# Attention probabilities of all four heads turned by 32x32 blocks and moved inside SBUF, instead of two by TensorE and two through DRAM

## The chip, the core and the metric

One core of one Trainium2 chip runs the whole program. The metric is the device time of one execution in microseconds (us); the kernel before is given as the median of three runs.

## What is computed

The input is x, 8 batches of 128 rows of 512 numbers. Stage one is a linear layer with a chosen low-rank adapter and an attention of 32 small heads. Stage three is a linear layer with a gate. The change lies in stage two, an attention with 32 query heads of 128, 8 key/value heads, and a paged cache of 512 old keys and values per batch. For every batch b and group g (one key/value head and its four query heads) it computes, cut to what matters:

```python
q, k, v = x1 @ Wq.T, x1 @ Wk.T, x1 @ Wv.T       # k and v: 128 new rows
q, k = rope(rmsnorm(q) * wq), rope(rmsnorm(k) * wk)
keys, values = concat(cache, k), concat(cache, v)  # 640 rows
p = softmax(mask(q @ keys.T) / sqrt(128))          # 128 x 640 per head
h += (p @ values) @ Wo_part
```

## The kernel before, in words

The order of the work is written out by hand. `slots` (L1180) calls, on each engine, one `slot(m, one, two, last)` for each of the 64 items m (8 groups g by 8 batches b). `one` and `two` are the items one and two ahead, whose queries and keys are prepared meanwhile; `last` is the item behind, whose probabilities are multiplied with the values; `before` is two behind. An engine works off its own list in order, and semaphores join the lists. All products are made of high and low halves (`_h`, `_l`), three matmuls for a full product.

In a slot TensorE (PE) does `scores(m, 1)`, `out(before, 2)` and `out(before, 3)`, `turn_q(one)`, `scores(m, 2)`, `values_of_highs(last)`, `scores(m, 3)`, `values_of_lows(last)`, `turn_new(one)`, `project_q(two)`, `out(last, 0)`, `out(last, 1)`, `scores(one, 0)` and `project_kv(two)`. Between them stand two `turn_probs`.

A head's scores (128 queries by 640 keys) lie in the PSUM banks 0 and 1. VectorE (DVE) takes `minima` (L1618: mask, scale, minimum, into `sm`), ScalarE (ACT) takes `exponent` (L1504: `sm` to `pf`). The result must be turned, keys onto partitions, before the product with the values:

- heads 2 and 3 (`BY_PE`): `turn_probs` on PE (L1347, five 128x128 transposes into banks 2 and 3), the high half by `high` on ACT (L1517), the low half by `low` on DVE (L1640);
- heads 0 and 1 (`BY_DMA`): `turn_blocks` on DVE (L1631, every 32x32 block turned), `blocks_away` on the SP queue to DRAM (L1246), `blocks_back` in four transfers of 80 KB (L1253) that put the blocks in their places, then `high_moved` on ACT (L1522) and `low_moved` on GpSimd (POOL, L1775), both over 640 columns.

The new key of `one` is turned by rope: DVE makes two products in `new_values` (L1600), POOL adds and scales them in `rope_keys` (L1758), PE turns the result in `turn_new` (L1330), ACT and DVE take its halves in `new_keys`. POOL also does `rms` (L1744: two small instructions, the second a power), the low halves of the cached keys and values (L1771, L1767), the rope sum of the queries (L1753), and the low halves of the next group's weights in the slots with b = 0, 1, 5 and 6.

The SP queue issues all transfers, in the order of `slot` at L1262: blocks, cached keys, blocks, cached values, weights.

## Time and profile before

| | |
|---|---|
| runs | 1300.37, 1301.07, 1304.16 us |
| median | 1301.07 us |
| span of the profiled execution, first to last instruction | 1299.0 us |
| busy: PE, DVE, ACT, POOL | 1249.3, 985.6, 837.8, 836.1 us |
| mean granted TensorE clock | 0.984 |

The page of the profiled execution gives its span and no other time of it; the median of the runs is 2.1 us above the span. Busy times are sums over the whole program; the second stage lies from about 265 to 1250 us. In a timeline each row has the start, the duration, the engine, the line of the kernel, the operation, and output<-inputs; what stands in brackets is how long the engine had been idle and what released it. Matmuls of PE are pipelined, so the durations of two that follow each other overlap, and what one costs is the distance between starts.

### The profile page before, as it was taken

To read this page: it belongs to the slowest core of one execution; us is meant where nothing else is said; L and a number is where in the kernel's file an instruction comes from. 1 tells how busy PE (TensorE), PEld (TensorE's weight loads), DVE (VectorE), ACT (ScalarE), POOL (GpSimd) and SP (SyncE) were. 2 spreads that over 40 slices of the span, in tenths; PEclk is the share of its full clock that TensorE was granted. 3 is DMA by queue.
4 is the path that set the end of the run, shared out by engine and by line. 5 is a ranking of instruction groups with operands and counts; after the bars stand their busy time and mean duration, and the time that the engine had idled before them with its cause. 6 is when DMAs were issued, how large, how long until landed. Compare 5 with 4: busy or idle time off the path is not lost. (4 is left out here: it accounts for less than half of the span.)

```text
span 1299.0 us, 26260 instructions
## 1 busy us (share of the span) xinstructions
PE 1249.3 (96%) x7496; PEld 1074.6 (83%) x7496; DVE 985.6 (76%) x2388; ACT 837.8 (64%) x2505; POOL 836.1 (64%) x787
## 2 busy tenths in 40 slices
PE   5799997799999999999999999999999999999988
PEld 4677775688888888888888888888888888888878
DVE  3567857467888878887888778878888888788766
ACT  2667777466767676666766776676666767666731
POOL 1656656475767676758665876687667766775741
PEclk9899998899999999999999999999999999999999
DMA  7546554345455555555555555555555455455441
GB/s 264 204 170 243 206 217 151 104 115 146 133 139 134 140 140 142 143 139 134 146 136 146 137 144 131 139 137 144 134 143 140 131 143 143 126 138 141 134 133 65
DMA packets 288945, 191.48 MB, mean 147 GB/s; under 512 B 151201, under 2 KB 256674, under 8 KB 287778
## 3 DMA queue, kind: packets, MB, share of 16 engines
q1 hardware_dynamic: 287792, 189.64, 51.2%
q8 instruction: 61, 1.00, 0.3%
q14 instruction: 82, 0.67, 0.2%
q10 hardware_dynamic: 1010, 0.17, 0.1%
HBM read 143.60 MB, written 79.69 MB: 172 GB/s over the span
## 5 line engine op out<-in xcount | busy, mean ns | idle before, releaser
L1779 POOL TENSOR_TENSOR b_p_l<-b_moved,b_p_h 128x640 fp32r<-128x640 f32 x128 | 200.9, 1570 | 163.9 <-PE ps L1375 93.8
L1514 ACT ACTIVATE b_pf<-b_sm,b_mn 128x640 f32<-128x640 f32 x256 | 212.4, 830 | 127.5 <-DVE b_mn L1624 127.5
L1624 DVE CUSTOM_DVE_ANT_0 b_sm<-ps,mask_row,b_rstd 128x640 f32<-128x640 f32 x256 | 225.0, 879 | 53.7 <-PE ps L1301 48.8
L1526 ACT ACTIVATE b_p_h<-b_moved 128x640 fp32r<-128x640 f32 x128 | 94.7, 740 | 160.0 <-DMA b_moved<-blocks_of_probs 158.8
L1660 DVE SCALAR_TENSOR_TENSOR b_hacc<-ps,b_ri,b_hacc 128x512 f32<-128x512 f32 x248 | 182.4, 736 | 4.6 <-PE ps L1301 4.3
L1299 PE MATMUL ps<-b_w_h,x1t_h 128*128 128x512 f32 (+1 forms) x512 | 178.8, 349 | 0.1
L1299 PE MATMUL ps<-b_kt_h,b_qt_h 128*128 128x320 f32 x512 | 169.5, 331 | 4.6 <-DVE b_mn L1624 4.2
L1300 PE MATMUL ps<-b_w_l,x1t_h 128*128 128x512 f32 (+1 forms) x512 | 173.4, 339 | 0.0
L1301 PE MATMUL ps<-b_w_h,x1t_l 128*128 128x512 f32 (+1 forms) x512 | 173.2, 338 | 0.0
L1301 PE MATMUL ps<-b_kt_h,b_qt_l 128*128 128x320 f32 x512 | 159.3, 311 | 0.0
L1300 PE MATMUL ps<-b_kt_l,b_qt_h 128*128 128x320 f32 x512 | 159.2, 311 | 0.0
L1644 DVE TENSOR_TENSOR b_p_l<-ps,b_p_h 128x640 fp32r<-128x640 f32 x128 | 104.8, 819 | 41.1 <-ACT b_p_h L1520 41.1
L1638 DVE STREAM_TRANSPOSE b_blk<-b_pf 128x640 f32<-128x640 f32 x128 | 107.8, 842 | 33.6 <-ACT b_pf L1514 33.6
L1769 POOL TENSOR_TENSOR b_v_l<-b_cv,b_v_h 128x512 fp32r<-128x512 f32 x64 | 82.9, 1295 | 57.0 <-ACT b_v_h L1496 56.9
L738 POOL TENSOR_TENSOR a_pr<-a_pr,a_ri 128x512 f32<-128x512 f32 x64 | 68.4, 1080 | 71.9 <-DVE a_ri L603 71.9
L1299 PEld LDWEIGHTS ps<-b_kt_h,b_qt_h 128*128 128x128 f32 x512 | 97.1, 190 | 13.0 <-DVE b_mn L1624 6.5
L1301 PEld LDWEIGHTS ps<-b_w_h,x1t_l 128*128 128x128 f32 x512 | 96.4, 188 | 11.8
L441 ACT ACTIVATE a_pr<-a_sm,a_mn 128x128 f32<-128x128 f32 x256 | 99.1, 397 | 10.7 <-PE ps L308 10.5
L1299 PEld LDWEIGHTS ps<-b_w_h,x1t_h 128*128 128x128 f32 x512 | 96.7, 189 | 9.6 <-issue 0.8
L1299 PE MATMUL ps<-b_wo_h,b_o_h 128*128 128x512 f32 x256 | 101.6, 397 | 2.7 <-DVE b_o_l L1648 1.6
L1300 PEld LDWEIGHTS ps<-b_w_l,x1t_h 128*128 128x128 f32 x512 | 96.8, 189 | 8.6
L1367 PE MATMUL ps<-b_p_h,b_v_l 128*128 128x512 f32 x256 | 102.3, 400 | 0.0
(177 smaller groups left out, 3371.1 us busy)
## 6 DMA issues: line engine op xcount, KB each, us to landing
blocks_of_probs<-b_blk SPq DMA_DIRECT2D x128, 320.0 KB, 2.4
b_moved<-blocks_of_probs SPq DMA_DIRECT2D x512, 80.0 KB, 2.1
kv_of_batch<-in_kv SPq DMA_DIRECT2D x128, 256.0 KB
b_ck<-kv_of_batch SPq DMA_DIRECT2D x64, 256.0 KB, 4.0
b_cv<-kv_of_batch SPq DMA_DIRECT2D x256, 64.0 KB, 1.9
raw<-in_w SPq DMA_DIRECT2D x32, 384.0 KB, 3.2
raw<-in_wo SPq DMA_DIRECT2D x32, 256.0 KB, 2.8
a_xt<-in_xt SPq DMA_DIRECT2D x8, 256.0 KB, 6.7
```

Source lines behind the costliest of these rows:

```text
L441: op = act.activation(pr[:, c % 4, j], sm[:, c % 2, j], ACT.Exp, bias=mn[:, h:h + 1], scale=-1.0, accum_out=rs[:, h:h + 1])
L1299: pe.matmul(out, lhs[0], rhs[0], start=start, stop=False)
L1300: pe.matmul(out, lhs[0], rhs[1], start=False, stop=False)
L1301: return pe.matmul(out, lhs[1], rhs[0], start=False, stop=stop)
L1367: mm = pe.matmul(ps[:, OT, :], l, p_h[:, i], start=False, stop=False)
L1514: act.activation(pf[:, h % 2], sm[:, h % 2], ACT.Exp, bias=mn[:, m.b % 2, h:h + 1], scale=-1.0, accum_out=rs[:, m.b % 2, h:h + 1]).then_in ...
L1526: act.activation(blocks_of(p_h[:, :, h * P:(h + 1) * P]), moved[:, d].rearrange("p (a t j) -> p a t j", a=LT, j=QUAD), ACT.Copy).then_inc( ...
L1624: dve.tensor_tensor_reduce(sm[:, h % 2], score_row, mask_row[:, m.b], rstd[:, m.b % 4, h:h + 1], -MASKED, ALU.add, ALU.min, mn[:, m.b % 2, ...
L1638: dve.transpose(by_quadrant(blk[:, d]), by_tile(pf[:, h % 2])).then_inc(blk_sb, 1)
L1644: dve.tensor_tensor(p_l[:, :, cols], turned_row, p_h[:, :, cols], ALU.subtract).then_inc(pl_sb, 1)
L1660: dve.scalar_tensor_tensor(out=hacc[:, m.b], in0=ps[:, OUT[h], :], scalar=share, in1=hacc[:, m.b], op0=ALU.mult, op1=ALU.add).then_inc(h_s ...
L1779: pool.tensor_tensor(blocks_of(p_l[:, :, h * P:(h + 1) * P]), moved[:, d].rearrange("p (a t j) -> p a t j", a=LT, j=QUAD), blocks_of(p_h[: ...
```

## The change

All four heads go one way. `turn_blocks` on DVE turns the blocks of each head and writes a pair of heads into one tile (`blk_first`, `blk_second`). `blocks_across` on the SP queue moves a pair in four transfers of 160 KB from SBUF to SBUF, each from 32 partitions to all 128, with no step through DRAM. ACT and POOL take the high and the low half of a pair in one instruction of 1280 columns each. The keys of a tile come out in another order (partition 4j + c has key 32c + j), so the cached values are loaded and the new keys written in that order.

The exponential writes over `sm`. `minima` of head h then waits until head h-2 has been turned on DVE, and `pf` is gone. The scores use two pairs of banks in turn. `scores(m, 3)` stands right behind `scores(m, 2)`. The sum of the two rope products of the new key moves from POOL to DVE (`key_sum`, both inputs in SBUF), and its scaling from POOL to ACT (`turned_key`). The low halves of the second pair are taken by POOL in the next slot, behind `rms`. Stage three's small tiles get other places.

```diff
+            def blocks_across(m, pair):
+
+                sp.wait_ge(blk_sb, REP * m.n + 2 * (pair + 1))
+                wait(sp, ml_sb, 2 * (m.n - 1) + pair + 1)
+                for a in range(LT):
+                    place = moved[:, pair].rearrange("p (h a n) -> p h a n", h=2, a=LT)[:, :, a]
+                    sp.dma_start(place, blk[pair][a * QUAD:(a + 1) * QUAD, :]).then_inc(moved_in[pair], 16)
 
             def slot(m, one, two, last):
-                if m:
-                    blocks_away(m, 0)
-                    blocks_back(m, 0)
-                    blocks_away(m, 1)
+                blocks_across(m, 0)
                 if two:
                     key_rows(two)
-                blocks_back(m, 1)
-                if two:
-                    value_rows(two)
...
+                blocks_across(m, 1)
+                if two:
+                    value_rows(two)
...
-                wait(pe, mn_sb, REP * m.n + h)
+                wait(pe, mn_sb, REP * m.n + h - 1)
                 q = slice(h * P, (h + 1) * P)
-                for bank, place, keys in ((SC, slice(LEAD, 512), slice(0, CUT)), (SC + 1, slice(0, CUT), slice(CUT, NK))):
+                first = SC[h % 2]
+                for bank, place, keys in ((first, slice(LEAD, 512), slice(0, CUT)), (first + 1, slice(0, CUT), slice(CUT, NK))):
...
-            def turn_probs(m, h):
-                pe.wait_ge(exp_sb, REP * m.n + h + 1)
-                wait(pe, pl_sb, len(BY_PE) * m.n + BY_PE.index(h))
-                for i in range(NT):
-                    mm = pe.transpose(turned_row[:, i], pf[:, h % 2, i * P:(i + 1) * P], ident[:])
-                mm.then_inc(pt_ps, 1)
...
                 scores(m, 2)
+                scores(m, 3)
                 if last:
                     values_of_highs(last)
-                scores(m, 3)
-                if last:
                     values_of_lows(last)
                 if one:
                     turn_new(one)
-                turn_probs(m, 2)
...
-                turn_probs(m, 3)
...
+            def turned_key(m):
+                act.wait_ge(kab2_sb, m.n + 1)
+                act.wait_ge(rstd_sb, m.n + 1)
+                act.activation(ka[:], kb[:], ACT.Copy, scale=rstd[:, m.b % 4, REP:REP + 1]).then_inc(kr_sb, 1)
...
+            def high(m, pair):
+                act.wait_ge(moved_in[pair], 16 * LT * (m.n + 1))
                 wait(act, pvh_ps, m.n)
+                act.activation(pair_of(p_h, pair), moved_pair(pair), ACT.Copy).then_inc(mh_sb, 1)
...
                 exponent(m, 2)
                 if m.b == 6:
                     kv_weights(m.g + 1)
-                high_moved(m, 0)
+                if one:
+                    turned_key(one)
                 if last:
                     output(last)
                 exponent(m, 3)
-                high(m, 2)
+                high(m, 0)
                 if one:
                     new_keys(one)
                     cache_values(one)
-                high_moved(m, 1)
...
+            def key_sum(m):
+                dve.wait_ge(kab_sb, m.n + 1)
+                dve.tensor_tensor(kb[:], ka[:], kb[:], ALU.add).then_inc(kab2_sb, 1)
...
                 if one:
                     new_values(one)
-                if last:
-                    low(last, 3)
+                    key_sum(one)
                 minima(m, 2)
                 turn_blocks(m, 1)
                 if before:
                     accumulate(before, 3)
                 if m.n == end.n:
                     h_rest(dve, 1)
+                minima(m, 3)
                 if one:
                     queries(one)
-                minima(m, 3)
+                turn_blocks(m, 2)
                 if last:
                     output(last)
                     invert(last)
-                low(m, 2)
+                turn_blocks(m, 3)
...
+            def low_probs(m, pair):
+                pool.wait_ge(mh_sb, 2 * m.n + pair + 1)
                 wait(pool, pv_ps, m.n)
+                pool.tensor_tensor(pair_of(p_l, pair), moved_pair(pair), pair_of(p_h, pair), ALU.subtract).then_inc(ml_sb, 1)
 
             def slot(m, one, two, last):
                 if one:
                     rms(one)
-                    rope_keys(one)
+                if last:
+                    low_probs(last, 1)
...
-                low_moved(m, 0)
+                low_probs(m, 0)
                 if one:
                     cache_values(one)
-                low_moved(m, 1)
```

The first place is DVE in an early slot, from the products of the new key to the first product of the queries. Of the kernel before:

```order
L1602 TENSOR_TENSOR b_vn_l<-ps,b_vn_h 128x128
L1605 TENSOR_TENSOR b_ka<-ps,cw 128x128
L1607 TENSOR_TENSOR b_kb<-ps,sw 128x128
L1644 TENSOR_TENSOR b_p_l<-ps,b_p_h 128x5x128
L1624 ISA b_sm,b_mn<-ps,mask_row,b_rstd 128x640
L1624 ISA b_mn 128x1
L1638 STREAM_TRANSPOSE b_blk<-b_pf 128x640
L1612 TENSOR_TENSOR b_qt_l<-ps,b_qt_h 128x512
L1624 ISA b_sm,b_mn<-ps,mask_row,b_rstd 128x640
```

And of the changed kernel:

```order
L1568 TENSOR_TENSOR b_vn_l<-ps,b_vn_h 128x128
L1571 TENSOR_TENSOR b_ka<-ps,cw 128x128
L1573 TENSOR_TENSOR b_kb<-ps,sw 128x128
L1578 TENSOR_TENSOR b_kb<-b_ka,b_kb 128x128
L1595 ISA b_sm,b_mn<-ps,mask_row,b_rstd 128x640
L1595 ISA b_mn 128x1
L1608 STREAM_TRANSPOSE b_blk_first<-b_sm 128x4x160
L1624 SCALAR_TENSOR_TENSOR b_hacc<-ps,b_ri,b_hacc 128x512
L1595 ISA b_sm,b_mn<-ps,mask_row,b_rstd 128x640
L1595 ISA b_mn 128x1
L1582 TENSOR_TENSOR b_qt_l<-ps,b_qt_h 128x512
L1608 STREAM_TRANSPOSE b_blk_second<-b_sm 128x4x160
```

The low half of head 3 has gone from its place behind `b_kb`, and the sum with two SBUF inputs stands there, ahead of the minima of head 2 and of everything that follows them.

The second place is POOL over one slot. Of the kernel before:

```order
L1749 TENSOR_SCALAR b_rstd<-b_ss 128x5
L1751 TENSOR_TENSOR b_rstd<-b_rstd,half 128x5
L1762 TENSOR_TENSOR b_ka<-b_ka,b_kb 128x128
L1765 TENSOR_SCALAR b_ka<-b_ka,b_rstd 128x128
L1773 TENSOR_TENSOR b_kt_l<-b_ck,b_kt_h 128x512
L1779 TENSOR_TENSOR b_p_l<-b_moved,b_p_h 128x4x5x32
L1769 TENSOR_TENSOR b_v_l<-b_cv,b_v_h 128x512
L1779 TENSOR_TENSOR b_p_l<-b_moved,b_p_h 128x4x5x32
L1756 TENSOR_TENSOR b_ra<-b_ra,b_rb 128x512
```

And of the changed kernel:

```order
L1712 TENSOR_SCALAR b_rstd<-b_ss 128x5
L1714 TENSOR_TENSOR b_rstd<-b_rstd,half 128x5
L1732 TENSOR_TENSOR b_p_l<-b_moved,b_p_h 128x8x5x32
L1727 TENSOR_TENSOR b_kt_l<-b_ck,b_kt_h 128x512
L1732 TENSOR_TENSOR b_p_l<-b_moved,b_p_h 128x8x5x32
L1723 TENSOR_TENSOR b_v_l<-b_cv,b_v_h 128x512
L1719 TENSOR_TENSOR b_ra<-b_ra,b_rb 128x512
```

The two instructions on the new key are gone, the low halves are twice as wide, and one of them stands right behind the power of `rms`.

## Rows read from the trace of the kernel before

**Rows 1.** Windows of 40 us, busy time of each engine, granted clock, DMA share.
```profile
280.00:320.00 40.00, 40.00 (x237) 35.52 (x236) 33.21 (x67) 26.00 (x76) 24.67 (x25) 1.00 0.51 134
...
1040.00:1080.00 40.00, 40.00 (x225) 34.93 (x225) 32.03 (x64) 25.71 (x70) 23.90 (x22) 1.00 0.56 143
```

**Rows 2.** Timeline of DVE from the rope of the queries on.
```profile
702.54 0.68 DVE L1598 TENSOR_TENSOR b_rb<-ps,sw 128x512 f32<-128x512 f32 x1
703.14 0.74 DVE L1660 SCALAR_TENSOR_TENSOR b_hacc<-ps,b_ri,b_hacc 128x512 f32<-128x512 f32 x1
704.34 0.88 DVE L1624 CUSTOM_DVE_ANT_0 b_sm<-ps,mask_row,b_rstd 128x640 f32<-128x640 f32 x1 [0.46 <-PE ps L1301]
...
706.22 0.84 DVE L1638 STREAM_TRANSPOSE b_blk<-b_pf 128x640 f32<-128x640 f32 x1 [0.33 <-ACT b_pf L1514]
707.18 0.88 DVE L1624 CUSTOM_DVE_ANT_0 b_sm<-ps,mask_row,b_rstd 128x640 f32<-128x640 f32 x1
...
707.99 0.75 DVE L1660 SCALAR_TENSOR_TENSOR b_hacc<-ps,b_ri,b_hacc 128x512 f32<-128x512 f32 x1
708.65 0.28 DVE L1602 TENSOR_TENSOR b_vn_l<-ps,b_vn_h 128x128 fp32r<-128x128 f32 x1
...
709.05 0.28 DVE L1607 TENSOR_TENSOR b_kb<-ps,sw 128x128 f32<-128x128 f32 x1
...
724.71 0.28 DVE L1607 TENSOR_TENSOR b_kb<-ps,sw 128x128 f32<-128x128 f32 x1
```

**Rows 3.** Timeline of PE: one `turn_probs`, the scores behind it, the lows.
```profile
705.42 0.71 PE L1351 MATMUL ps<-ident,b_pf 128*128 128x128 f32 x5
705.88 0.39 PE L1299 MATMUL ps<-b_kt_h,b_qt_h 128*128 128x320 f32 x1
706.11 0.31 PE L1300 MATMUL ps<-b_kt_l,b_qt_h 128*128 128x320 f32 x1
706.26 0.31 PE L1301 MATMUL ps<-b_kt_h,b_qt_l 128*128 128x320 f32 x1
...
712.78 1.09 PE L1375 MATMUL ps<-b_p_l,b_v_h 128*128 128x512 f32 x4
```

**Rows 4.** Timeline of POOL in the second stage.
```profile
702.70 1.57 POOL L1779 TENSOR_TENSOR b_p_l<-b_moved,b_p_h 128x640 fp32r<-128x640 f32 x1 [0.16 <-ACT b_p_h L1526]
704.24 1.29 POOL L1756 TENSOR_TENSOR b_ra<-b_ra,b_rb 128x512 f32<-128x512 f32 x1
706.63 0.20 POOL L1749 TENSOR_SCALAR b_rstd<-b_ss 128x5 f32<-128x5 f32 x1 [1.11 <-ACT b_squares_out L1475]
706.91 1.19 POOL L1751 TENSOR_TENSOR b_rstd<-b_rstd,half 128x5 f32<-128x5 f32 x1
...
730.96 2.40 POOL L1737 TENSOR_TENSOR b_w_l<-raw,b_w_h 128x1024 fp32r<-128x1024 f32 x1
```

**Rows 5.** Timeline of DVE in the first stage: instructions with both inputs in SBUF.
```profile
80.42 1.07 DVE L572 TENSOR_TENSOR a_qr<-a_rope_a,a_rope_b 128x512 f32<-128x512 f32 x1
...
94.11 0.68 DVE L871 TENSOR_TENSOR sw<-t_minus_sine,t_norms 128x512 f32<-128x512 f32 x1
```

**Rows 6.** Timeline of POOL in the first stage, at the same times.
```profile
79.90 1.04 POOL L738 TENSOR_TENSOR a_pr<-a_pr,a_ri 128x512 f32<-128x512 f32 x1
80.90 1.75 POOL L724 TENSOR_TENSOR a_kr<-a_rope_a,a_rope_b 128x512 f32<-128x512 f32 x1
```

**Rows 7.** Timeline of the SP queue: four transfers from DRAM back, one head.
```profile
709.27 1.74 SPq L1260 DMA_DIRECT2D b_moved<-blocks_of_probs  x4
```

**Rows 8.** DMA issues of the page: KB of each, median us from issue to landing.
```profile
b_moved<-blocks_of_probs SPq DMA_DIRECT2D x512, 80.0 KB, 2.1
...
b_ck<-kv_of_batch SPq DMA_DIRECT2D x64, 256.0 KB, 4.0
```

**Rows 9.** Timeline of ACT: copies of 640 and of 1024 columns.
```profile
712.60 0.74 ACT L1526 ACTIVATE b_p_h<-b_moved 128x640 fp32r<-128x640 f32 x1 [0.78 <-DMA b_moved<-blocks_of_probs]
...
727.45 1.05 ACT L1456 ACTIVATE b_w_h<-raw 128x1024 fp32r<-128x1024 f32 x1
```

More of the change, by code:

```diff
@@ L932, in phase3 @@
     ht_h, ht_l = (x1t_l[:, 4], x1t_l[:, 5]), (x1t_l[:, 6], x1t_l[:, 7])
-    b_gate = sb("b_gate", [P, NR])
-    first = sb("first", [P, NR])
+    b_gate, first = small_rows[:, 0:NR], small_rows[:, NR:2 * NR]
+    sc, weight = [small_rows[:, 8 * (1 + i):8 * (2 + i)].rearrange("p (k r) -> p k r", k=2) for i in range(2)]
+    top, expert = small_rows[:, 24:26], small_rows[:, 26:28]
     most = sb("most", [P, 2, MAXR])
-    sc = sb("sc", [P, 2, NR])
-    top = sb("top", [P, 2])
-    weight = sb("weight", [P, 2, NR])
-    expert = sb("expert", [P, 2])
-    low = sb("low", [P, 2, 2, MAXR])
     lowt = sb("lowt", [P, 2, P], F32R)
@@ L948, in phase3 @@
     bth_sb, btl_sb = sem("bth_sb"), sem("btl_sb")
-    small = ((b_gate, "b_gate"), (first, "first"), (most, "most"))
+    small = ((b_gate, "b_gate"), (first, "first"), (most[:], "most"))
     def flat(ap):
@@ L1074, in choose @@
         dve.wait_ge(top_sb, b + 1)
-        dve.scalar_tensor_tensor(out=weight[:, k], in0=sc[:, k], scalar=top[:, k:k + 1], in1=first[:],
+        dve.scalar_tensor_tensor(out=weight[:, k], in0=sc[:, k], scalar=top[:, k:k + 1], in1=first,
                                  op0=ALU.is_ge, op1=ALU.mult).then_inc(weight_sb, 1)
@@ L1155, in phase2 @@
         hacc = sb("hacc", [P, B, D])
[L1156 to L1157 removed]
+        blk_second = sb("blk_second", [P, 2 * NK])
+        blk = (blk_first, blk_second)
+        moved = sb("moved", [P, 2, 2 * NK])
         const_sb = sem("const_sb")
@@ L1170, in phase2 @@
         mn_sb, exp_sb, ri_sb = sem("mn_sb"), sem("exp_sb"), sem("ri_sb")
-        ph_sb, pl_sb = sem("ph_sb"), sem("pl_sb")
-        blk_sb, blk_out, moved_in = sem("blk_sb"), [sem(f"blk_out{h}") for h in BY_DMA], [sem(f"moved_in{h}") for h in BY_DMA]
+        blk_sb, moved_in = sem("blk_sb"), [sem(f"moved_in{pair}") for pair in range(2)]
         mh_sb, ml_sb = sem("mh_sb"), sem("ml_sb")
@@ L1212, in blocks_of, with pair_of, moved_pair, head_in_pair @@
         def blocks_of(ap):
-            return ap.rearrange("p t (a j) -> p a t j", a=LT)
+            return ap.rearrange("p t (b j) -> p b t j", j=QUAD)
+        def pair_of(tile, pair):
+            return blocks_of(tile[:, :, pair * 2 * P:(pair + 1) * 2 * P])
+        def moved_pair(pair):
+            return moved[:, pair].rearrange("p (b t j) -> p b t j", b=2 * LT, j=QUAD)
+        def head_in_pair(h):
+            return blk[h // 2][:].rearrange("p (c h t j) -> p h c t j", c=LT, h=2, j=QUAD)[:, h % 2]
+        def by_block(ap):
+            return ap.rearrange("p (j c) -> p c j", c=LT)
         block = ctx.enter_context(nc.Block())
@@ L1541, in slot @@
                 if last:
-                    high(last, 3)
+                    high(last, 1)
                 exponent(m, 1)
@@ L1579, in slot @@
                     exponent(one, 0)
-            scalar_first(act, (q_weights, kv_weights, squares, new_kv, queries, cache_keys, new_keys, cache_values))
+            scalar_first(act, (q_weights, kv_weights, squares, new_kv, queries, turned_key, cache_keys, new_keys, cache_values))
             slots(act, slot)
-            high(end, 3)
+            high(end, 1)
             h_out(act, 2)
@@ L1710, in low_kv_weights @@
                 dve.tensor_tensor(w_l[:, :, cols], raw[:, :, cols], w_h[:, :, cols], ALU.subtract).then_inc(wkvl_sb, 1)
-            vector_first(dve, (rope_products, new_values, queries, new_keys, minima, low_weights, low_kv_weights))
+            vector_first(dve, (rope_products, new_values, key_sum, queries, new_keys, minima, low_weights, low_kv_weights))
             slots(dve, slot)
             accumulate(end.before(), 2)
-            low(end, 3)
             accumulate(end.before(), 3)
@@ L1808, in _ @@
             pool.wait_ge(const_sb, 1)
-            gpsimd_first(pool, (q_weights, kv_weights, rope_queries, rms, rope_keys, cache_keys, cache_values))
+            gpsimd_first(pool, (q_weights, kv_weights, rope_queries, rms, cache_keys, cache_values))
             slots(pool, slot)
+            low_probs(end, 1)
             pool_ffn(pool)
```

116 lines of the change are left out of this document (29 added, 87 removed).

## Prediction

> **What bounds it now.** I read the windows first. From 280 to 1080 us PE is busy for 40.00 of every 40 us, twenty windows long, at a clock of 1.00 [rows 1]. DVE is busy for 32 to 33 of them, ACT and POOL for 24 to 30. The timelines then give the period: `b_kb` starts at 709.05 and again at 724.71, so a slot takes **15.66 us** [rows 2], and 64 of them are nearly the whole second stage. PE never waits in a slot. So whatever PE is spared is won in full, as long as no other engine needs more than the new slot. That condition is what has to be worked out.
>
> **What PE is spared.** Five turns take 0.46 us (705.42 to 705.88), and the matmul behind them holds the next one for 0.23 us where its like takes 0.15 (705.88 to 706.11, 706.11 to 706.26) [rows 3]. That is 0.54 per `turn_probs`, 1.09 for two. `turn_new`, which stood ahead of one of them, now pays its own 0.08. PE saves 1.0 us, and its slot would be **14.65 us**; over some 62 slots that is -62 us. The second pair of score banks and the moved `scores(m, 3)` issue the same matmuls and remove no wait, since there is none: nothing.
>
> **DVE.** Per slot two `low` of 640 columns go and two block turns of 0.84 us come [rows 2], both about 0.75 from start to start: nothing. `key_sum` is new, 128 columns like `b_kb`, 0.20 from start to start. DVE then needs about 12.7 of 14.65 us.
>
> **ACT.** Four copies of 640 columns become two of 1280. A copy takes 0.74 for 640 and 1.05 for 1024 columns [rows 9], so 1.26 for 1280, an estimate along that line: a little less in all. `turned_key`, 128 columns, comes in. ACT stays under 11 us of a slot; nothing by itself.
>
> **POOL.** A low half takes 1.57 for 640 columns, 1.29 goes for 512 and 2.40 for 1024 [rows 4]. Along that line 1280 columns take 2.96, and the next starts after 2.93. Two of them, three instructions of 1.27 (keys, values, rope sum of the queries) and `rms` with the power (0.37 and 1.18) make 11.2 us. Weights add 12.6 us in eight slots (eight pieces of 1.27 and one of 2.4). That is 12.8 of 14.65 on average, but in slots 0, 5 and 6 of each group it runs over, and the next `low_probs(last, 1)` is late.
>
> **The transfers.** Per pair four transfers of 160 KB replace, for two heads, a trip to DRAM and eight transfers of 80 KB. Four take 1.74 us to issue, 1.31 to the start of the last [rows 7]. From issue to landing the near row says 2.1 us (80 KB), the far one 4.0 (256 KB, of smaller packets) [rows 8]; I take 2.4, near the first, since the packets keep their kind and only their number doubles. The Trainium skill gives a reason for more ("SBUF — State Buffer", Door 1: The DMA port swizzle): of SBUF's 16 DMA ports 32 partitions reach only 8, and it states 189 GB/s measured there. By that figure, as an estimate, four such transfers need 3.5 us, and the landing would be 3.5. No row here shows a read from 32 partitions.
>
> **The wait that the change brings.** In the second stage no DVE instruction of before has both inputs in SBUF. In the first stage some do, and there the rows show what happens beside POOL. Such an instruction of 512 columns takes 0.68 us (L871) [rows 5]. The one at 80.42 took 1.07: POOL was inside an instruction from 79.90 to 80.94, and the DVE one ended 0.55 after that [rows 5, 6]. POOL's next instruction, begun at 80.90, in turn took 1.75. So whoever is first holds the other up to its end. The Trainium skill says the same as a rule ("SBUF — State Buffer", Who interferes with whom): a DVE instruction with two SBUF inputs and a GpSimd one that reads SBUF exclude each other for the whole instruction; the trace agrees, with those 0.39 us.
>
> `key_sum` is just such an instruction, and POOL now has instructions of 2.96 us. Count from the start of `scores(m, 1)` in a slot of 14.65 us. `b_kb` starts 3.2 to 3.4 us in, so `key_sum` is ready at 3.6. On POOL the first pair's low half begins when ACT has copied it (about 10.9), then values and rope sum, so `rms` starts at 1.7 of the next slot, the power at 1.95 and `low_probs(last, 1)` at 3.15. It is first by 0.45 us and holds DVE until 6.1, **2.5 us**. DVE has only 2 us to spare in a slot, and behind `key_sum` are queued the minima of head 2, all turns, `queries` and the rope products. `project_q` waits for `queries`, `turn_new` for ACT's `turned_key`.
>
> Once that happens the slot is set by a loop, whose pieces are: `key_sum` 0.20, minima 0.81, turn of head 1 0.84, to the queue 0.04, fourth transfer 1.31 later, landing 2.4, ACT 0.04 and 1.26, POOL 0.07 and 2.93 (low half of the first pair), 1.27, 1.25, `rms` 0.37, power 1.18, low half of the second pair 2.96, and then `key_sum` again. **The sum is 16.9 us.** In the weight slots POOL is late enough for `key_sum` to slip in ahead, but then PE waits for the lows, needed 6.8 us into the slot [rows 3] (712.78 less 705.88), some 2.6 us; those slots take 16.3 to 17.3. The mean is 16.75, +1.1 against 15.66, or **+68 us** over 62 slots. The end adds about 2, since the last pair's way (transfer, two long halves) is longer than that of a PE turn. Against the span of 1299 that is 1369, and the runs' median is 2 above the span: **1371 us**.
>
> How sure is it that POOL is first? In the loop both ways start from ACT's copy of the first pair. POOL's takes 8.33 us (1.26, 0.07, 2.93, 1.27, 1.25, 0.37, 1.18). DVE's is: copy 1.15, the new key's halves 0.50, rope 1.21, accumulate 0.66, minima to turn 1.88, turn 0.76, minima 0.81, accumulate 0.66, three small ones 0.71 [rows 2]; 8.34. That is a tie. When `key_sum` wins it waits only for the power, the next slot is again one of 14.65, and in it POOL is first by 0.45 us. So at least every second slot is held up.
>
> **Rivals.**
> - **Every second slot only.** `key_sum` wins the tie, or the transfers land so late (3.2 and more) that POOL begins behind it. Slots of 14.65 to 15.3 and of 17 in turn, a mean near 16.1: +27, 1328 us (1306 to 1340). For it: the tie. Against it: with the landing at 2.1 to 2.6 POOL keeps its lead after each free slot.
> - **No hold-up worth naming**, the other side: `key_sum` costs its 0.20 us. Then POOL alone costs something: `low_probs(last, 1)` would end at 6.2, the lows are needed at 6.8, and 2.5 us of weights make PE wait 1.9 twice a group, and `turn_q` 1.5 once for the rope sum, 5.3 us in eight slots or 0.66 each. The slot is 15.3, -0.35, or 1280 us. It decides whether POOL's instruction is under way at 3.6 us; the held instructions of the first stage speak against it. With a landing of 3.5 this case too comes to 15.6 and no difference.
> - **The full gain**, 14.65 us a slot, 1239 us: needs POOL's wide halves under 2.5 us besides; the rows of 1024 columns exclude nearly that.
> - **Late landing with the hold-up.** By rows the bound is the 4.0 of `b_ck`, a loop of 18.5 us and over 1412; I keep only part of that in the range, as a late landing also hands the tie to `key_sum`. (The port figure of the Trainium skill, landing 3.5, would make the loop 18.0.)
>
> **Chances.** Forecast 0.50 (1340 to 1412), every second slot 0.25, worse than 1412 0.04, no hold-up 0.12, full gain 0.03, and 0.06 for a draw. A measurement of this kernel tells 0.3% (4 us) from no change. So faster 0.15, same 0.06, slower 0.79. The range, 1295 to 1412, leaves out about 0.14 below and 0.04 above; the forecast's own is 1340 to 1412.
>
> **What would show it.** PE no longer at 40.00 of 40 us; slots near 16.9. `key_sum` of over 2 us by its duration, ending with POOL's wide low half; PE idle before `project_q` behind DVE's `b_qt_l` and before `turn_new` behind ACT's `b_ka`. POOL's wide instruction near 2.96, ACT's near 1.26, the transfers landing after 2.4. It is wrong if `key_sum` takes 0.2 to 0.3 us in most slots, or if POOL's wide instruction starts after it.

## The result and the profile after

The changed kernel takes **1418.16 us** (median of four runs, 1401.18 to 1428.49) against 1301.11 us, 117 us more; the forecast was 1371 and its range ended at 1412. The ratio is 1.086, with an interval of 1.079 to 1.093: it leaves out the run of 1428.49 us, which counts as slow, and without it the median is 1414.6 us and the differences from the changed kernel given below would be some 4 us smaller. The profiled execution took 1401.18 us, with a span of 1399.4; it was the fastest of its kernel, so the profile shows 100 of the 117 us.

Windows of the changed kernel, the columns as in [rows 1]:

```profile
280.00:320.00 40.00, 34.73 (x188) 28.88 (x187) 32.35 (x58) 21.61 (x63) 24.54 (x16) 1.00 0.54 126
1040.00:1080.00 40.00, 36.99 (x199) 31.00 (x198) 31.25 (x64) 27.76 (x76) 34.79 (x24) 0.96 0.52 121
```

PE is no longer busy for 40 of 40 us. From one sine product of the queries on DVE (`b_rb`) to the next, 58 slots between 280 and 1300 us took 15.8 to 19.4 us, 17.3 in the mean, where before they took 15.7. What PE and DVE waited for, between 300 and 1260 us (us in total, times, longest):

```profile
PE ps L1358 <- POOL b_p_l L1732: 31.5, 17, 2.2
PE ps L1290 <- DVE b_kt_l L1587: 28.8, 35, 1.6
PE ps L1290 <- DVE b_qt_l L1582: 18.1, 15, 1.2
PE ps L1323 <- ACT b_ka L1467: 8.2, 11, 0.8
...
DVE b_kt_l L1587 <- ACT b_kt_h L1476: 108.5, 55, 3.3
```

The third and fourth row are the two waits that the forecast named behind a held `key_sum`. The second was not foreseen. PE waits there for the low half of the new key on DVE, and DVE waits (last row) for its high half on ACT: that copy, L1476, stands behind ACT's wide copy, which waits for the transfer.

Two slots of POOL and DVE from the timelines, one held and one free:

```profile
697.51 1.18 POOL L1714 TENSOR_TENSOR b_rstd<-b_rstd,half 128x5 f32<-128x5 f32 x1
698.66 2.95 POOL L1732 TENSOR_TENSOR b_p_l<-b_moved,b_p_h 128x1280 fp32r<-128x1280 f32 x1
698.71 3.04 DVE L1578 TENSOR_TENSOR b_kb<-b_ka,b_kb 128x128 f32<-128x128 f32 x1
701.68 0.87 DVE L1595 CUSTOM_DVE_ANT_0 b_sm<-ps,mask_row,b_rstd 128x640 f32<-128x640 f32 x1
...
716.39 1.18 POOL L1714 TENSOR_TENSOR b_rstd<-b_rstd,half 128x5 f32<-128x5 f32 x1
717.51 0.29 DVE L1578 TENSOR_TENSOR b_kb<-b_ka,b_kb 128x128 f32<-128x128 f32 x1
717.78 0.88 DVE L1595 CUSTOM_DVE_ANT_0 b_sm<-ps,mask_row,b_rstd 128x640 f32<-128x640 f32 x1
717.90 2.97 POOL L1732 TENSOR_TENSOR b_p_l<-b_moved,b_p_h 128x1280 fp32r<-128x1280 f32 x1 [0.33 <-ACT b_p_h L1493]
```

At 698.71 POOL is first by 0.05 us, and `key_sum` takes 3.04 us instead of 0.29. At 717.51 it is itself first and takes 0.29; POOL's wide instruction starts 0.39 later, when ACT has copied the second pair. Of the 64 instances of `key_sum` 20 take over 1 us, 29 take 0.29, and 15 take 0.52 to 0.59, these beside POOL's weight instructions. Between 280 and 1300 us slots with a held `key_sum` take 18.0 to 19.4 us, 18.5 in the mean; most of the others without weights take 15.8 to 16.1.

The way of one pair, from the SP queue to ACT's wide copy:

```profile
703.34 2.91 SPq L1254 DMA_DIRECT2D b_moved<-b_blk_first  x4
706.30 0.61 SPq L1240 DMA_DIRECT2D b_ck<-kv_of_batch  x1
706.95 2.01 SPq L1232 DMA_DIRECT2D raw<-in_w  x1
709.06 2.62 SPq L1254 DMA_DIRECT2D b_moved<-b_blk_second  x4
...
709.19 1.28 ACT L1493 ACTIVATE b_p_h<-b_moved 128x1280 fp32r<-128x1280 f32 x1 [3.48 <-DMA b_moved<-b_blk_first]
```

From the first issue to the copy this is 5.85 us, where the forecast had 1.31 + 2.4 + 0.04 = 3.75. The fourth transfer started 2.0 us after the first and landed 3.8 later. In the median of all first pairs it is 2.0 and 3.6. Of the page's list of transfers (median us to landing last), to be set beside [rows 8]:

```profile
b_moved<-b_blk_first SPq DMA_DIRECT2D x256, 160.0 KB, 3.3
b_moved<-b_blk_second SPq DMA_DIRECT2D x256, 160.0 KB, 3.3
```

### The profile page after: what moved, and what is told of

The parts are those of the page before. It is cut to its first block, busy times and chain, and to the rows that moved or that the text cites. A ratio compares the mean times of both kernels' runs of the same rounds, so it can differ in the third digit from the quotient of the medians.

```text
span 1399.4 us, 23898 instructions
## 1 busy us (share of the span) xinstructions
PE 1243.0 (89%) x6856; PEld 1012.9 (72%) x6856; DVE 1042.1 (74%) x2452; ACT 846.4 (60%) x2441; POOL 943.2 (67%) x659
## 4 chain that ended last, share of the span: by engine, by line
PE 29%; POOL 27%; DMA 13%; issue 9%; DVE 7%; SPq 7%; ACT 6%; DVEq 0%; POOLq 0%; ACTq 0%
POOL b_p_l L1732 13%; DMA b_moved<-b_blk_first 12%; SPq L1254 7%; PE ps L1290 4%; ACT b_p_h L1493 4%; PE ps L1291 4%; PE ps L1292 4%; POOL b_v_l L1723 4%; POOL b_ra L1719 3%; DVE b_blk_first L1608 3%; PE ps L247 2%; POOL b_w_l L1694 2%; PE ps L1358 2%; DVE b_sm L1595 2%; PE ps L306 2%
## 5 line engine op out<-in xcount | busy, mean ns | idle before, releaser
L1732 POOL TENSOR_TENSOR b_p_l<-b_moved,b_p_h 128x1280 fp32r<-128x1280 f32 x128 | 380.9, 2976 | 292.7 <-ACT b_p_h L1493 292.5
L1487 ACT ACTIVATE b_sm<-b_sm,b_mn 128x640 f32<-128x640 f32 x256 | 212.3, 829 | 98.6 <-DVE b_mn L1595 94.0
L1493 ACT ACTIVATE b_p_h<-b_moved 128x1280 fp32r<-128x1280 f32 x128 | 163.2, 1275 | 134.3 <-DMA b_moved<-b_blk_first 111.1
L1290 PE MATMUL ps<-b_w_h,x1t_h 128*128 128x512 f32 (+1 forms) x512 | 190.2, 372 | 24.1 <-DVE b_qt_l L1582 24.0
L1608 DVE STREAM_TRANSPOSE b_blk_first<-b_sm 128x640 f32<-128x640 f32 x128 | 107.7, 842 | 34.5 <-ACT b_sm L1487 34.4
L1587 DVE TENSOR_TENSOR b_kt_l<-ps,b_kt_h 128x128 fp32r<-128x128 f32 x64 | 18.7, 292 | 129.5 <-ACT b_kt_h L1476 129.5
L1448 ACT ACTIVATE b_squares_out<-ps 128x128 bf16<-128x128 f32 x256 | 67.5, 278 | 76.5 <-DVE b_rb L1564 76.5
L1358 PE MATMUL ps<-b_p_l,b_v_h 128*128 128x512 f32 x256 | 80.5, 439 | 36.8 <-POOL b_p_l L1732 36.6
L1498 ACT ACTIVATE b_o_h<-ps 128x512 fp32r<-128x512 f32 x64 | 38.0, 594 | 119.0 <-PE ps L1358 119.0
L1608 DVE STREAM_TRANSPOSE b_blk_second<-b_sm 128x640 f32<-128x640 f32 x128 | 106.5, 833 | 1.4
```

Of the source, the lines that this page charges most:

```text
L1290: pe.matmul(out, lhs[0], rhs[0], start=start, stop=False)
L1358: mm = pe.matmul(ps[:, OT, :], h, p_l[:, i], start=False, stop=i == LT)
L1487: act.activation(sm[:, h % 2], sm[:, h % 2], ACT.Exp, bias=mn[:, m.b % 2, h:h + 1], scale=-1.0, accum_out=rs[:, m.b % 2, h:h + 1]).then_in ...
L1493: act.activation(pair_of(p_h, pair), moved_pair(pair), ACT.Copy).then_inc(mh_sb, 1)
L1608: dve.transpose(head_in_pair(h), by_tile(sm[:, h % 2])).then_inc(blk_sb, 1)
L1732: pool.tensor_tensor(pair_of(p_l, pair), moved_pair(pair), pair_of(p_h, pair), ALU.subtract).then_inc(ml_sb, 1)
```

## The experiments

Three causes were on the table: `key_sum` held up by POOL, the late landing (by its source partitions or by its issues), and POOL's load with the wide low halves and the weights. In every one the time is the median, the ratio is to the kernel before in the same session, and waits of PE are taken between 300 and 1260 us.

**e1, `key_sum` with one input in SBUF.** It reads the key in PSUM instead of the sine part, which is thus left out.

```diff
-                dve.tensor_tensor(kb[:], ka[:], kb[:], ALU.add).then_inc(kab2_sb, 1)
+                dve.tensor_tensor(kb[:], ps[:, PJK, 0:HD], ka[:], ALU.add).then_inc(kab2_sb, 1)
```

> The changed kernel, but key_sum takes its first input from PSUM (the unturned key) instead of the product in SBUF: same size, same place, same waits, one SBUF input instead of two. It leaves the sine part of the new keys' rope out, so its output is another. Theory H (the hold-up by POOL is most of the loss): key_sum takes 0.3 us in every slot, and the time falls to 1301 or below, near 1280. Theory T (the pair transfers, 5.8 us from the first issue to the landing instead of the 3.7 forecast, are most of it): slots of 15.8 and up remain, and the time is 1350 to 1365, so the hold-up is worth 45 to 60 us.

Measured: 1358.0 us, ratio 1.042 (1.040 to 1.044). The line of `key_sum` (shortest, median and longest ns), changed kernel first, then e1:

```profile
L1578 DVE TENSOR_TENSOR b_kb<-b_ka,b_kb x64: 291/530/3103, 231.0 to 1326.6; 128x128 f32<-128x128 f32 x64
```

```profile
L1578 DVE TENSOR_TENSOR b_kb<-ps,b_ka x64: 290/291/293, 231.7 to 1285.5; 128x128 f32<-128x128 f32 x64
```

The hold-up is real and goes with the second SBUF input. It is worth 60 us, about half of the loss, not all of it. The slots that are left take at least 15.8 us, as expected of the late transfers.

**e2, the transfers read from all 128 partitions.** The same bytes and packets, but each transfer takes a quarter of the columns of every partition instead of all columns of 32 partitions; the blocks land in wrong places.

```diff
-                    sp.dma_start(place, blk[pair][a * QUAD:(a + 1) * QUAD, :]).then_inc(moved_in[pair], 16)
+                    sp.dma_start(place, blk[pair][:, a * 2 * NT * QUAD:(a + 1) * 2 * NT * QUAD].rearrange("p (h n) -> p h n", h=2)).then_inc(moved_in[pair], 16)
```

> The changed kernel, but each of the four transfers of a pair reads a quarter of the columns of all 128 partitions instead of all columns of 32 partitions; bytes, number of transfers, pieces of 640 bytes and destination stay. The blocks land in wrong places, so its output is another. If the reading of 32 partitions limits the transfers: landing falls from 3.3 to about 2.4 us, and the time by 50 us or so, to about 1365 (the hold-up stays). If it is the number of pieces or the form of the destination: landing and issue (0.62 us each) stay, and the time stays at 1400 to 1420.

Measured: 1366.2 us, ratio 1.048 (1.043 to 1.053). Of e2's list of transfers:

```profile
b_moved<-b_blk_first SPq DMA_DIRECT2D x256, 160.0 KB, 2.3
b_moved<-b_blk_second SPq DMA_DIRECT2D x256, 160.0 KB, 2.9
```

A source of 32 partitions costs the first pair 1.0 us of landing and the second 0.4, and the kernel 52 us. In e2 the first pair's landing is what the forecast assumed (its fourth transfer lands after 2.4 us), and so is the result: 1366 us against 1371, slots of 16.7 in the mean against 16.75. They come in the way of the first rival, though, free ones of 14.7 among held ones of 17 to 18.5: `key_sum` takes over 1 us in 27 of 64 places.

**e3, both edits.**

> Both edits together, one input of key_sum from PSUM and transfers that read all partitions; output as in those two. Theory T: hold-up gone and landing 2.4 us, the time is 1285 to 1305. Theory H without a part of the transfers: 1280, the same as with the one-input edit alone. If neither edit shortens the transfers: as with the one-input edit alone.

Measured: 1304.1 us, ratio 1.0016 (1.0005 to 1.0027). The gains add up: 60 and 52 alone, 114 together. What is left of PE's waits:

```profile
PE ps L1358 <- POOL b_p_l L1732: 33.9, 19, 2.2
PE ps L1318 <- POOL b_ra L1719: 4.9, 4, 1.2
```

Most plain slots take 14.6 to 15.2 us, so PE's saving of 1.0 is there. Slots with weights take 16.5 to 18.1. The mean is 15.7, that of before.

**e4, e3 with the values in the partitions of before.**

```diff
-                    sp.dma_start(cv[q::LT], rows_of).then_inc(cv_in, 16)
+                    sp.dma_start(cv[q * PSIZE:(q + 1) * PSIZE], rows_of).then_inc(cv_in, 16)
```

> As the run before, and the cached values are loaded into 32 partitions in a row as in the kernel before, not into every fourth (they then meet the wrong keys, so its output is another). If every-fourth placing costs the queue its time, the issue of b_cv falls from 0.61 to 0.43 us and the issue of the four transfers behind it can start earlier: up to 5 us less. If not: no difference in time.

Measured: 1303.0 us, ratio 1.001 (0.9995 to 1.0025). An issue of `cv` takes 0.43 us again instead of 0.60, and it is worth nothing that the runs can tell (1.1 us): SP's queue seems to have room at that place.

**e5, a `key_sum` that leaves nothing out.** The sine product goes to free columns of the key's PSUM bank and is read there.

```diff
-                dve.tensor_tensor(kb[:].rearrange("p (t d) -> p t d", t=2), turned,
+                dve.tensor_tensor(ps[:, PJK, 2 * HD:3 * HD].rearrange("p (t d) -> p t d", t=2), turned,
...
-                dve.tensor_tensor(kb[:], ka[:], kb[:], ALU.add).then_inc(kab2_sb, 1)
+                dve.tensor_tensor(kb[:], ps[:, PJK, 2 * HD:3 * HD], ka[:], ALU.add).then_inc(kab2_sb, 1)
```

> The same sum as the changed kernel, but the sine part of the new key's product is written to four hundred bytes of the free columns of the key's score bank (PJK, columns 256 to 383) and key_sum reads it there, so that it has one input from SBUF only and nothing is left out. If what e1 won (1418 to 1358 us) came from the hold-up by POOL alone, this gives 1358 us (1353 to 1363), with key_sum at 0.29 to 0.31 us in every slot. Rival: that e1 won by leaving a product's result unused (the write and read of kb overlapping less), or that a product written to PSUM takes longer than the 0.24 us it takes now; then key_sum still falls to 0.3 us but the time stays above 1365.

Measured: 1354.6 us, ratio 1.040 (1.036 to 1.043), `key_sum` at 0.29 us in all 64 places. So the whole gain of e1 is to be had in a kernel that computes everything, and leaving the sine out had no part in it.

**e6, e5 with another order of a pair's transfers.**

```diff
-                for a in range(LT):
+                for a in (0, 2, 1, 3):
```

> As e5, with the four transfers of a pair issued in the order a = 0, 2, 1, 3, so that neighbours in time read partitions 64 apart instead of 32. If two transfers that overlap hinder each other because their source partitions lie beside each other, the landing falls below the 3.3 us of the changed kernel, by up to 0.5 us, and the time by up to 15 us against e5. If each is slow by its own 32 source partitions (e2 brought 2.2 to 2.4 us with 128), the order changes nothing: within 4 us of e5.

Measured: 1338.4 us, ratio 1.028 (1.025 to 1.030), 16 us less than e5 for an order of four numbers. In e5 both pairs land after 3.3 us, in e6:

```profile
b_moved<-b_blk_first SPq DMA_DIRECT2D x256, 160.0 KB, 3.0
b_moved<-b_blk_second SPq DMA_DIRECT2D x256, 160.0 KB, 3.2
```

Neighbouring quarters do hinder each other. The Trainium skill gives the map ("SBUF — State Buffer", Door 1: The DMA port swizzle): partitions 32 apart share their ports, those 64 apart do not, so of the quarters 0 and 1 use one half of the ports, 2 and 3 the other. The measurement agrees in direction; how many ports were at work no trace here shows.

**e7, e3 without most of the low halves of the weights.** POOL makes 8 columns of each piece from group 1 on.

```diff
-                    pool.tensor_tensor(w_l[:, c, 0:D], raw[:, c, 0:D], w_h[:, c, 0:D], ALU.subtract).then_inc(wql_sb, 1)
+                    pool.tensor_tensor(w_l[:, c, part(g)], raw[:, c, part(g)], w_h[:, c, part(g)], ALU.subtract).then_inc(wql_sb, 1)
```

> e3 (sum with one input, transfers from all 128 partitions; the sine part left out of the key and the blocks landing in wrong places) and, besides, the low halves of the weights of groups 1 to 7 cut to 8 of 512 columns on POOL, so that every slot has POOL at 11.6 us at most. If what holds e3 at the time of before (1304 us) is POOL's work in the weight slots 0, 1, 5 and 6 alone, the slots all go at TensorE's 14.65 to 14.8 us: 64 x (16.5 to 18.0 in four slots of eight, to 14.8) gives back 32 x about 2.3 = 74 us less, some of which ACT's own weight copies keep: 1240 us (1230 to 1255), with no stretch at half clock left but few. Rival: that the wide low halves of 2.95 us hold TensorE in plain slots too, or that ACT's weight copies are what makes those slots long: then 1270 to 1300.

Measured: 1258.8 us, ratio 0.966 (0.963 to 0.968), and of PE's 33.9 us behind the lows 0.4 are left:

```profile
PE ps L1290 <- DVE b_kt_l L1587: 3.6, 4, 1.0
...
PE ps L1358 <- POOL b_p_l L1735: 0.4, 1, 0.4
```

Slots take 15.0 us in the mean. The third term is thus 45 us: wide low halves and weights together are too much for POOL in the weight slots. Some of it may be the clock's, which the next run looks at: the stretches at the low level fall from 27 us in e3 to 4 in e7. The expectation of 1240 was 19 too low, outside its own range.

**e8, waits of PE filled.** Four transposes ahead of the first scores, four products ahead of the lows, all unneeded.

```diff
+                for i in range(4):
+                    pe.matmul(ps[:, OT, :], v_l[:, m.b % 2, i], p_h[:, i], start=False, stop=False)
                 pe.wait_ge(ml_sb, 2 * (m.n + 1))
...
+                    wait(pe, mn_sb, REP * m.n - 1)
+                    for _ in range(4):
+                        pe.transpose(ps[:, SC[0], 0:P], ident[:], ident[:])
                     pe.wait_ge(qtl_sb, m.n + 1)
```

> The changed kernel with TensorE work that nobody needs in front of two of its waits: four 128-column transposes before the first scores of an item, and four 512-column products (a low value by a high probability, which adds a small part twice) before the values of the lows, some 0.7 and 0.9 us. TensorE had about 2.6 us of idle time in a slot. If the stretches of 3.4 us at 1.2 GHz (19 of them, 64.8 us) come after idle time and cost about 32 us of the 1418, most go and the time falls to 1395 (1385 to 1410), less whatever the filling itself delays. Rival: the low clock falls into time in which TensorE would have waited anyway and costs nothing; then the stretches go, and the time stays or rises by the filling in the slots that TensorE bounds: 1418 to 1450.

Measured: 1412.6 us (1410.8 to 1414.3), ratio 1.084 (1.081 to 1.086), between the expected range and the rival's. This was about TensorE's clock. In the held slot above, the changed kernel's windows of 3 us show (length of the window and PE's busy time first, the granted clock third from the end):

```profile
701.00:704.00 3.00, 2.25 (x11) 1.45 (x9) 3.00 (x6) 1.41 (x4) 1.91 (x2) 1.00 0.00 0
704.00:707.00 3.00, 1.78 (x6) 1.33 (x6) 3.00 (x7) 1.21 (x3) 0.00 (x0) 0.85 0.67 132
707.00:710.00 3.00, 3.00 (x9) 2.36 (x9) 0.49 (x1) 0.81 (x1) 0.00 (x0) 0.58 1.09 198
```

PE idles for 0.75 and 1.22 us behind ACT's `b_ka` and DVE's `b_qt_l`, and then runs at 1.2 GHz for a while. Products of 512 columns start 0.43 us apart there, and 0.23 apart where the clock is back at 2.4 GHz; two of each:

```profile
706.25 0.63 PE L1290 MATMUL ps<-b_w_h,x1t_h 128*128 128x512 f32 x1
706.68 0.63 PE L1291 MATMUL ps<-b_w_l,x1t_h 128*128 128x512 f32 x1
...
709.84 0.39 PE L1290 MATMUL ps<-b_wo_h,b_o_h 128*128 128x512 f32 x1
710.07 0.40 PE L1291 MATMUL ps<-b_wo_l,b_o_h 128*128 128x512 f32 x1
```

Windows of 3 us laid end to end from 280 to 1290 us add up to some 61 us at that level in the changed kernel, to none in the kernel before, and to none in e8. By those steps 61 us at the low level take at most some 28 us of PE's time, an estimate that holds if PE had work throughout. But with the low clock gone e8 stands only 6 us below the changed kernel's median, inside the spread of its runs. The filling costs something too, and `key_sum` is held in 25 of 64 places instead of 20. So the low clock is a companion of the waits here; a price for it by itself is not shown.

**e9, the new keys ahead of the wide copy on ACT.** The changed kernel with this alone:

```diff
                 exponent(m, 3)
-                high(m, 0)
                 if one:
                     new_keys(one)
+                high(m, 0)
+                if one:
                     cache_values(one)
```

> The changed kernel with two calls of ACT's slot exchanged: the copy of the new keys (0.26 us, its input ready some 2 us earlier) stands ahead of the wide copy of the first pair, which waits for the transfer. In the changed kernel VectorE then sat idle for that copy, 114 us in 57 slots between 300 and 1300 us, and TensorE's first scores behind it. If the late landing costs its time through this queue on ACT, VectorE's wait of 2.0 us a slot goes, the slots become some 1.3 us shorter where POOL allows it (its work is 12.8 us a slot on average), and the time falls to 1345 (1320 to 1370). Rival: that the landing holds the loop through POOL's low halves and TensorE's low values instead; then VectorE's wait goes, idle time of the same size turns up ahead of the low values, and the time stays at 1400 to 1420.

Measured: 1373.7 us, ratio 1.055 (1.053 to 1.058), 4 above the range: 44 us for the place of a 0.26 us instruction. DVE's wait for `b_kt_h`, 108.5 us, is gone, and a new one stands first at PE:

```profile
PE ps L1318 <- POOL b_ra L1720: 48.0, 40, 2.3
PE ps L1358 <- POOL b_p_l L1733: 30.9, 18, 2.2
```

Not all of the 44 us is that wait. `key_sum` is held in 10 of 64 places instead of 20, so a part of it may be the hold-up's once more; the two are not separated here.

**e10, e6 with the exchange of e9.**

> e6 (key_sum with one input from SBUF, transfers in the order 0, 2, 1, 3; 1338 us) with the exchange of e9 on ACT. In e6 VectorE waited 1.80 us (704.20) and 2.51 us (720.33) for the copy of the new keys. If that wait is worth what it was in e9's theory, the slots without weights come down to TensorE's 14.7 to 15.0 us and the weight slots to 16.5: 1275 (1260 to 1300), so faster than the 1301 us of before. Rival: POOL's chain from the first pair's low halves to the second's (2.95, 1.30, 1.30, 1.4, 2.97 us) holds the low values of TensorE: 1305 to 1330.

Measured: 1336.2 us, ratio 1.028 (1.025 to 1.031): 2 us under e6, which the runs cannot tell from none. With the hold-up gone and the other order, the exchange of e9 brings nothing. The rival was right that POOL's chain holds PE, but it gave 1330 at most, and it named the low values, where PE waits 30.2 us. The larger wait is another. The landing now reaches PE by POOL, where `rope_queries` stands behind the wide low half and the low half of the values; PE waits for it 43.1 us in 48 places.

**e11, a part of the weights' low halves on DVE**, pieces 1 and 3 of the queries' and the output weights, with semaphores of their own (here one of the two functions and its places):

```diff
+            def low_out_weights(g, c):
+                dve.wait_ge(woh_sb, KT * g + c + 1)
+                dve.tensor_tensor(wo_l[:, c], raw[:, c, 0:D], wo_h[:, c], ALU.subtract).then_inc(wod_sb, 1)
...
+                if m.b == 1:
+                    low_out_weights(m.g, 3)
                 turn_blocks(m, 2)
...
                     accumulate(last, 1)
+                if m.b == 0:
+                    low_out_weights(m.g, 1)
```

> e10, and the low halves of weight pieces 1 and 3 (out weights of every group, query weights of groups 1 to 7) made by VectorE instead of POOL: four pieces of 512 columns a group, 1.2 us each on POOL, 0.7 us on VectorE, one in each of the slots 0, 1, 5 and 6. e7 without these low halves gained 45 us on e3, so half of that work moved should give 15 to 20 us: 1258 (1245 to 1280) where e10 is at 1275. Rival: VectorE, which works 12.2 us of a slot, is delayed itself by 0.7 us or more in each of the 32 slots, two-input instructions from SBUF that wait for POOL's 2.95 us among them: no gain, or 10 to 40 us more than e10.

Measured: 1316.7 us, ratio 1.012 (1.009 to 1.016). The difference to e10 is the 20 us expected, from a level that was not. PE's two largest waits:

```profile
PE ps L1333 <- POOL b_ra L1754: 47.6, 53, 1.6
PE ps L1373 <- POOL b_p_l L1767: 16.9, 19, 2.2
```

The wait for the low probabilities is halved, that for the queries' sum stays.

**e12, e10 with two of a pair's four transfers issued by ACT.**

```diff
+            def blocks_too(m, pair):
+                act.wait_ge(blk_sb, REP * m.n + 2 * (pair + 1))
+                wait(act, ml_sb, 2 * (m.n - 1) + pair + 1)
+                for a in (2, 3):
...
+                    act.dma_start(place, blk[pair][a * QUAD:(a + 1) * QUAD, :]).then_inc(moved_in[pair], 16)
```

> e10, with transfers 2 and 3 of each pair issued by ACT (those of the first pair ahead of its output copy, those of the second behind the wide copy of the first pair) and 0 and 1 by SP, so that the four starts take 0.6 instead of 1.9 us where both queues are free. If the late landing still holds the loop in e10, the landing comes 1.2 us earlier and the time falls by 5 to 30 us against e10. Rival: the issue costs ACT itself 0.6 us or more for each of four, 2.4 us a slot of the 10 us that it works, or it waits there for VectorE with its output copy behind it: 10 to 80 us slower than e10.

Measured: 1344.2 us, ratio 1.034 (1.031 to 1.038), 8 us slower than e10 in the median, with spreads of 10 and 5 us. Its list of transfers:

```profile
b_moved<-b_blk_first SPq DMA_DIRECT2D x128, 160.0 KB, 3.3
b_moved<-b_blk_first ACTq DMA_DIRECT2D x128, 160.0 KB, 3.9
```

Started closer together, they land later, 3.3 and 3.9 us against 3.0 in e10. The fourth starts 0.7 us after the first instead of 2.0, but from the first issue to the last landing the first pair takes 5.4 us in the median, in e10 5.3. What earlier starts would bring is lost in the landing: the transfers share something. That ACT has the issues in its own list may cost a part of the 8 us; the two were not separated.

**e13 and e14, the values ahead of the first pair.** e13 is e11 with `cache_values(one)` ahead of `high(m, 0)` on ACT and ahead of `low_probs(m, 0)` on POOL, which in e11 had idled there for 3.7 us in the mean; e14 moves `rope_queries(two)` ahead too.

```diff
-                low_probs(m, 0)
                 if one:
                     cache_values(one)
+                low_probs(m, 0)
                 if two:
                     rope_queries(two)
```

> e11 (1317 us) with the cache's values ahead of the first pair on both engines: ACT copies their high half ahead of its wide copy of the first pair, POOL makes their low half ahead of its wide low half of the first pair, where POOL stood idle for 4 to 5 us. In e11 TensorE waited 47.6 us in 53 places for the turned queries' sum on POOL, which stood behind both. With one instruction of 1.3 us less between the landing and that sum, most of the wait goes: 1316.7 - 45 = 1272 (1262 to 1290), faster than before. Rival: the wait only moves to the low values of TensorE (POOL's second wide low half) or to VectorE's blocks: 1300 to 1320.

> As e13, and POOL's sum for the next but one item's queries ahead of the wide low half of the first pair as well. TensorE's wait for it is then gone altogether, but POOL waits for VectorE's products where the transfer lands early, and the wide low halves start up to 1.3 us later. If the queries' sum is what holds the loop: at or below e13, 1255 to 1275. Rival: the low values of TensorE wait for POOL's second wide low half instead: above e13, 1280 to 1310.

Measured: e13 **1268.5 us**, ratio 0.975 (0.973 to 0.977); e14 1269.0 us, ratio 0.975 (0.973 to 0.978). Both compute everything that the reference does, and both are faster than the kernel before by 2.5%. Windows and PE's waits of e13:

```profile
280.00:320.00 40.00, 40.00 (x224) 34.66 (x223) 35.17 (x72) 27.18 (x77) 30.95 (x20) 1.00 0.60 142
1040.00:1080.00 40.00, 39.01 (x209) 32.81 (x208) 35.47 (x73) 30.20 (x73) 32.92 (x22) 1.00 0.55 134
```

```profile
PE ps L1373 <- POOL b_p_l L1766: 17.9, 22, 2.0
PE ps L1333 <- POOL b_ra L1753: 5.5, 11, 1.4
```

PE is back at 40.00 of 40 us in the early stretch, now mostly with slots of 14.5 to 14.9 where there is no weight, and 15.1 in the mean. The wait for the queries' sum fell from 47.6 to 5.5 us, though the transfers land as late as in e6, after 3.0 and 3.2 us. PE's waits of e14:

```profile
PE ps L1373 <- POOL b_p_l L1766: 14.9, 27, 2.1
PE ps L1305 <- DVE b_mn L1610: 7.0, 14, 0.5
```

In e14 the wait for the queries' sum is gone altogether, but 7.0 us behind DVE's minima have come, and the time is equal. What remains in both is the wait behind the low probabilities.

## Why the prediction was right and wrong

**Right.** The side, and the mechanism behind half of the loss: `key_sum` with two inputs in SBUF against POOL's long instruction, first come, first served, at the place in the slot that the working gave (3.4 us into it for `b_kb`, 3.7 for `key_sum`), and with the tie that it named; in the rows it is decided by 0.05 us one way and 0.39 the other. POOL's wide instruction was put at 2.96 us and took 2.98 in the mean; ACT's was put at 1.26 and took 1.28. PE's spared 1.0 us was right: most free slots of e2 and plain ones of e3 take 14.65 to 14.8. The waits behind a held `key_sum` (`b_qt_l`, `b_ka`) were the ones named.

**Wrong: the landing of 2.4 us.** This is the mis-sized term. "I take 2.4, near the first, since the packets keep their kind and only their number doubles" looked at bytes and packets and not at where a transfer reads. It measured 3.3, and 3.6 for the fourth transfer of the first pair, which is the one that the sum counts; the port figure of the Trainium skill, which the sum did not use, had said 3.5. e2, with 2.3, came out at 1366 us; so 52 us hang on this term, and with the landing as assumed the forecast would have been 5 us off (in part by luck, see below). The range held the landing only in part ("I keep only part of that in the range, as a late landing also hands the tie to `key_sum`"). The tie was handed over indeed, and the time was still above: the free slots were then not of 14.65 but of 15.8 to 16 us, for a reason that the working had not looked at: it followed the transfer to POOL, and not to what stood behind it on ACT. `new_keys`, 0.26 us, waited there for a transfer that it has nothing to do with, DVE waited for it 108.5 us and PE 28.8 us behind DVE, and e9 got 44 us for its place. How much of the free slots' 1.2 us this wait makes is not shown: e9's free slots still took 15.7 in the mean, now behind the queries' sum.

**Wrong: the fourth start 1.31 us after the first.** An issue took 0.62 us instead of 0.43, and the last began 2.0 us after the first. e12 speaks against a price of its own for that, since with starts 0.7 us apart the last transfer landed no earlier; but it also put issues into ACT's list, so the two are not told apart cleanly.

**Wrong in count: "So at least every second slot is held up".** The hold-up came in a third of the slots (20 of 64 over 1 us, 29 at 0.29), and such a slot took 18.5 us instead of 16.9, with the landing of the fourth transfer later by 1.2 and its start by 0.7. After a free slot the working had POOL first by 0.45 us; in the run up to four free slots stand in a row. The first rival had the pattern, two kinds of slots, and even the condition, "the transfers land so late (3.2 and more) that POOL begins behind it"; but its slots of both kinds were too short, and so was its 1328 us. The rival of a late landing with the hold-up, given 0.04, had the length of the held slots, 18.5 by the row of `b_ck`, but not that most slots would be free of it. With the hold-up and the landing in their places the mean came out alike by luck: e2's 16.7 is made of slots of 14.7 and of 17 to 18.5, held in 27 of 64 places, and its starts were still 2.0 us apart.

**Wrong: 1280 us without a hold-up.** The second rival gave that for a landing of 2.4. That kernel is e3, and it took 1304. POOL's load in the weight slots was about right: it was priced at 0.66 us a slot, and by e7 it is 45 us, 0.7 a slot. The remaining 20 us are there in e7 as well, whose slots take 15.0 us and not 14.65. They lie with waits that the working left at nothing, and are not settled further. Low clock was another unforeseen companion, 27 us of it in e3; its price is open, as said under e8.

Two readings of rows were off, and neither bears on the sum: the lows are needed 6.9 us into the slot (712.78 less 705.88), not 6.8, and POOL is busy for up to 32.4 of 40 us between 280 and 1080 us, not 30.

Put together: PE was spared 62 us and the kernel lost 117, so 179 us had to come from elsewhere. Three things were undone one by one: the hold-up (60 us), the sources of 32 partitions (52), the weights' low halves on POOL beside the wide ones (45). That is 157; the remaining 22 are the 0.35 us by which e7's slots (15.0 in the mean) stand above 14.65. The shares depend on what else is mended: e9's 44 us is another way to undo a part of the same loss, and e13 undoes all of it with the sources left at 32 partitions.

## What to carry to other kernels

When a transfer gets slower, look at every engine that waits for it and at what stands behind that wait in its own order: here 0.26 us of unrelated work was worth 44 us in one kernel and 2 in another, where the same lateness came back through the next queue. The gain came once the orders on ACT and POOL were mended and some of POOL's work had gone to DVE. Before long instructions of POOL are made longer, give every DVE instruction beside them no more than one input in SBUF; here a product left in PSUM did it at no cost that shows (e5). Price an SBUF-to-SBUF transfer by its source partitions too, and let neighbours in time read from different halves.

## What was not expected of the hardware

- 160 KB from 32 partitions of SBUF landed after 3.3 us, from 128 partitions after 2.3 in the first pair and 2.9 in the second, with the same packets and destination. The order 0, 2, 1, 3 of the four gave 3.0 and 3.2, and starting them two by two from two queues 3.3 to 3.9.
- A few nanoseconds decide which of the two engines is held. In the changed kernel both start at 750.29 in the rows, in the trace POOL at 750.286 and DVE at 750.289, and DVE is held for 3.10 us. In e2 both start at 703.34, DVE at 703.335 and POOL at 703.342, and POOL pays, 3.12 us instead of 2.96. Where the starts differ by 1 or 2 ns, either engine is the one held. The rows:

```profile
750.29 2.95 POOL L1732 TENSOR_TENSOR b_p_l<-b_moved,b_p_h 128x1280 fp32r<-128x1280 f32 x1
750.29 3.10 DVE L1578 TENSOR_TENSOR b_kb<-b_ka,b_kb 128x128 f32<-128x128 f32 x1
```

```profile
703.34 0.29 DVE L1578 TENSOR_TENSOR b_kb<-b_ka,b_kb 128x128 f32<-128x128 f32 x1
703.34 3.12 POOL L1732 TENSOR_TENSOR b_p_l<-b_moved,b_p_h 128x1280 fp32r<-128x1280 f32 x1
```

- The issue of `cv` on SP takes 0.60 us into every fourth partition and 0.43 into partitions in a row (e3 and e4). That is not the only thing that matters: the issue of `b_ck`, with no change of form, went from 0.43 us in the kernel before to 0.61 in the changed one, and of `raw<-in_w` from 0.43 to 1.8 (the 2.01 us above, ahead of the second pair). What these cost is not shown.
- After idle times of 0.75 and 1.22 us close together PE ran at 1.2 GHz for some 3 us, and filling part of its waits removed that wholly.
